# A fused transformer-like block: program parting moved to the end, more slack in the planned order, two blocks normalised on GpSimd

## The reference

```
h = tanh(xn @ W1.T + b1);  s = h @ w2.T + b2          # a score for each token
e = exp(s - max over the sequence)
ctx = cumsum(e * xn) / cumsum(e)                       # running mean along the sequence
attn = tanh(concat(ctx, xn) @ Wc.T + bc)
ffn = (silu(xn @ wg.T) * (xn @ wu.T)) @ wd.T           # wg, wu: 768 x 256, wd: 256 x 768
```

## Time and profile before

| | us |
|---|---|
| median of three runs | 396.42 |
| the profiled execution, whole | 396.52 |
| its span, first to last instruction | 394.3 |
| TensorE's first and last matmul | 1.5, 390.8 |
| flag written, branches on all engines | 67.9, 68.1 to 69.1 |
| VectorE busy, ScalarE busy, GpSimd busy | 296.4, 249.9, 192.2 |

### The profile page before, as it was taken

The page is one execution under the profiler, slowest core; times in us unless marked ns, Lnnn a source line. Parts: engine busy times, 40 slices in busy tenths (PEclk is TensorE's granted clock), DMA queues, the critical chain, the costliest instruction groups (busy, mean ns, idle before and its releaser), DMA issues.

```text
span 394.3 us, 7886 instructions
## 1 busy us (share of the span) xinstructions
PE 386.4 (98%) x2740; PEld 268.6 (68%) x2740; DVE 296.4 (75%) x632; ACT 249.9 (63%) x466; POOL 192.2 (49%) x257
## 2 busy tenths in 40 slices
PE   8999999999899999999999999999999999999996
PEld 4556676758566686777777776767677676676765
DVE  6799998999899989766848666788576765654351
ACT  4786898699787767797546836365463644536350
POOL 0535441273428997896825504947356555502000
PEclk9999999999999999999999999999999999999999
DMA  7933436037449324247330005142331330100001
GB/s 252 355 115 62 102 90 169 9 72 171 100 118 183 113 57 109 98 127 131 100 80 28 27 28 143 50 117 71 82 71 44 100 108 3 53 28 28 28 27 61
DMA packets 54946, 36.57 MB, mean 93 GB/s; under 512 B 31858, under 2 KB 50292, under 8 KB 54900
## 3 DMA queue, kind: packets, MB, share of 16 engines
q1 hardware_dynamic: 54608, 35.73, 34.0%
q10 hardware_dynamic: 292, 0.26, 0.2%
HBM read 20.19 MB, written 8.45 MB: 73 GB/s over the span
## 4 chain that ended last, share of the span: by engine, by line
PE 87%; DVE 6%; ACT 2%; issue 1%; SPq 1%; DMA 1%; POOL 0%; ACTq 0%; DVEq 0%; POOLq 0%
PE bank L686 41%; PE bank L722 36%; PE bank L742 8%; PE bank L1361 1%; SPq L1267 1%; DVE bank L1105 1%; DMA xres<-in_x 1%; DVE stats L940 1%; DVE ex L1110 1%; DVE bank L1090 1%; DVE veps L969 1%; ACT xt L838 1%; ACT xt L848 0%; DVE rstd L972 0%; DVE minus_half L970 0%
## 5 line engine op out<-in xcount | busy, mean ns | idle before, releaser
L722 PE MATMUL bank<-xt,narrow 128*128 128x512 f16 x768 | 177.8, 379 | 0.5 <-issue 0.5
L722 PEld LDWEIGHTS bank<-xt,narrow 128*128 128x128 f16 x768 | 75.1, 98 | 75.8 <-issue 1.0
L686 PE MATMUL bank<-narrow,wide 128*128 128x256 f16 x792 | 96.4, 273 | 0.0
L686 PE MATMUL bank<-narrow,xt 128*128 128x256 f16 x768 | 92.8, 273 | 0.0
L874 ACT ACTIVATE wide<-bank 128x512 f16<-128x512 f32 x90 | 53.6, 596 | 60.1 <-DVE bank L1105 59.7
L686 PEld LDWEIGHTS bank<-narrow,xt 128*128 128x128 f16 x768 | 75.1, 98 | 18.3 <-issue 0.4
L686 PEld LDWEIGHTS bank<-narrow,wide 128*128 128x128 f16 x792 | 77.5, 98 | 9.4
L1110 DVE TENSOR_TENSOR wide<-bank,wide 128x512 f16<-128x512 f32 x90 | 60.9, 683 | 25.1 <-ACT wide L874 24.2
L1105 DVE SCALAR_TENSOR_TENSOR bank<-bank,sg 128x512 f32<-128x512 f32 x96 | 66.1, 693 | 16.0 <-PE bank L722 15.6
L1235 POOL TENSOR_TENSOR wide<-ex,wide 128x512 f16<-128x512 f32 x32 | 39.4, 1246 | 78.8 <-ACT wide L888 78.7
L867 ACT ACTIVATE sg<-bank 128x512 f32<-128x512 f32 x96 | 56.7, 595 | 25.1 <-PE bank L722 24.2
(11 more groups left out here) (101 smaller groups left out, 263.9 us busy)
## 6 DMA issues: line engine op xcount, KB each, us to landing
rows<-scratch SPq DMA_DIRECT2D x16, 512.0 KB, 5.4
out_y<-xres SPq DMA_DIRECT2D x31, 256.0 KB, 2.2
xres<-in_x SPq DMA_DIRECT2D x15, 512.0 KB, 4.9
xt<-xt SPq DMA_TRANSPOSE x56, 2.5
wide<-in_wg SPq DMA_DIRECT2D x1, 768.0 KB, 6.5
wide<-in_wu SPq DMA_DIRECT2D x1, 768.0 KB, 8.9
wide<-in_wd SPq DMA_DIRECT2D x1, 768.0 KB, 10.6
wide<-in_wc SPq DMA_DIRECT2D x1, 512.0 KB, 11.8
```

The costliest lines, as they stand in the source:

```text
L686: return pe.matmul(dst, lhs, rhs, start=False, stop=stop, skip_group_check=True)
L722: mm = pe.matmul(b[:, :], pg.up(which, k, j), pg.xn(sx, k, tok), start=n == 0, stop=n == len(todo) - 1)
```

## The change

- The branch of an engine now waits in the plan for its last large step as well: D(15,2) on TensorE, Ct(15,2) on ScalarE, Da(15,0) on VectorE, Cl(15,1) on GpSimd, O(15,0) on SyncE. All steps may stand before it but Da and O of (15,1) and (15,2). The wide program repeats all, and loads all of x and all weights again (21 loads in place of 5).
- Steps Kg to Fl get due times from 215 on (they were 41 to 58) and come behind C(3,1); their copies lie in a part of `xt` that is free by then. K1 and Kc stay.
- In the plan, a result of another engine counts as seen 1.0 us later on TensorE and 0.3 us later on ScalarE, from 30 us on. On the engine that made it, it still counts 0.1 us sooner.
- Blocks 1 and 2 are normalised on GpSimd (new step Lp, a tensor_scalar with two per-partition factors), not on ScalarE.
- Load Lx(i) stands behind Tx(i-6), and counts as seen after 9.0 us; statistics are due 2 us sooner; block 2's x counts as there at 20.0.
- All orders are planned anew with this.

```diff
+SLACK, STEADY = {TE: 1.0, SE: 0.3}, 30.0
...
-    "T": (PO, 1.35, 1.45), "N": (PO, 3.2, 3.3), "Cl": (PO, 1.2, 1.3), "Xm": (PO, 1.5, 1.6),
+    "T": (PO, 1.35, 1.45), "N": (PO, 3.2, 3.3), "Cl": (PO, 1.2, 1.3), "Lp": (PO, 0.75, 0.85), "Xm": (PO, 1.5, 1.6),
...
-    "Lx": (SY, 0.6, 4.0), "Tx": (SY, 2.6, 4.8),
+    "Lx": (SY, 0.6, 9.0), "Tx": (SY, 2.6, 4.8),
...
+POOLED = (1, 2)
...
-X_SENT = (0.0, 11.1, 18.0)
+X_SENT = (0.0, 11.1, 20.0)
...
-AHEAD = ("Ln", "Lb", "Xh", "Xl", "Xm", "Tx", "Ss", "S", "Th", "Sv", "Gg", "Sg", "Gu", "H", "Hh", "Hl", "D", "Da")
+AGAIN = ("Ln", "Lp", "Lb", "Xh", "Xl", "Xm", "Tx", "Ss", "S", "Th", "Sv", "Gg", "Sg", "Gu", "H", "Hh", "Hl", "D", "Da",
+         "V0", "M1", "V1", "Ex", "M2", "V2", "M3", "V3", "Er", "Ro", "N", "Sc", "Ch", "Cl", "Cs", "C", "Ct", "Ca", "O")
+END = {TE: "D", SE: "Ct", VE: "Da", PO: "Cl", SY: "O"}
...
-                lead = 4.0 if i <= FIRST_T + 2 else 8.0
+                lead = 6.0 if i <= FIRST_T + 2 else 10.0
...
+            if i in POOLED:
+                due["Lp", i, pr] = due["Ln", i, pr]
...
+    for e, branch in BRANCH_OF.items():
+        if kind == branch:
+            return [(("Fl", 0, 0), 0), ((END[e], LAST, {TE: 2, SE: 2, VE: 0, PO: 1, SY: 0}[e]), 0)]
...
-        return [(("Tx", i - 5, 1), 0)] if i >= FIRST_T + 5 and not wide else []
+        return [(("Tx", i - 6, 1), 0)] if i >= FIRST_T + 6 and not wide else []
...
-    return kind in WEIGHTS + ONCE or (kind in AHEAD and i < BLK_SEQ - 1)
+    return kind in WEIGHTS + ONCE or (kind in AGAIN and not (kind in ("Da", "O") and st[1] == LAST and st[2]))
...
-            t = max(t, when - into - (0.1 if by == e else 0.0))
+            t = max(t, when - into + (-0.1 if by == e else SLACK.get(e, 0.0) if when > STEADY else 0.0))
...
-            return rows[:, :, :, :].rearrange("p r k t -> p (r k t)").bitcast(F16)[:, n * SHARE:(n + parts) * SHARE]
+            return xt[:, :].bitcast(F16).rearrange("p (c t) -> p c t", c=2 * KD)[:, n:n + parts, 2 * BLK:2 * BLK + SHARE]
...
+            elif kind == "Lp":
+                if i > FIRST_T + 1:
+                    pool.wait_ge(g_xm, pg.nth("Xm", i - 2, k))
+                elif i <= FIRST_T:
+                    pool.wait_ge(p_x, pg.nth("Lb", i - 1, k))
+                pool.wait_ge(*root_ready(i))
+                for t in range(2):
+                    c = 4 * i + 2 * k + t
+                    ins = pool.tensor_scalar(normed(pg, i, k)[:, t, :], xres[:, c, :], rstd[:, c:c + 1], shift[:, c:c + 1],
+                                             ALU.mult, ALU.add)
+                ins.then_inc(g_xn, 1)
```

More of the change, by code:

```diff
@@ L222, with norm @@
 DUE = due_times()
+def norm(i, wide):
+    return "Lp" if i in POOLED and not wide else "Ln"
 def needs(st, wide):
@@ L342, in __init__ @@
         self.earlier = {st[0]: 0 for st in DUE}
-        once = [st for st in earlier if st[0] in ONCE or st[0] not in AHEAD]
+        once = [st for st in earlier if st[0] in ONCE or st[0] not in AGAIN]
         for st in earlier:
@@ L351, in __init__ @@
         self.free = dict(BEGIN)
-        skip = {*self.done, *(st for st in DUE if not (st[0] not in WEIGHTS + ("Xm", "Tx") if wide else
+        skip = {*self.done, *(st for st in DUE if not (st[0] not in WEIGHTS + ("Xm", "Tx", "Lp") if wide else
                                                        st[1] < FIRST_T if st[0] in ("Lb", "Xl") else
                                                        st[1] >= FIRST_T if st[0] in ("Xm", "Tx") else
-                                                       st[:2] != ("Ln", 0)))}
+                                                       st[:2] != ("Ln", 0) and (st[0] not in ("Ln", "Lp") or st[0] == norm(st[1], wide))))}
         self.todo = {e: sorted((st for st in DUE if STEP[st[0]][0] == e and st not in skip), key=DUE.get)
@@ L585, in __init__ @@
                 self.plan = ANY if wide_operands else FITS
+                self.softmaxes, self.loads = (SEQS, NBLK // 2) if wide_operands else (0, 0)
                 if wide_operands:
@@ L799, in tensor_step, with through @@
                 mm.then_inc(p_m, 1)
+        def through(eng, pg):
+            eng.wait_ge(p_d, pg.plan.earlier["D"])
+            eng.wait_ge(a_y, pg.plan.earlier["Ct"])
+            eng.wait_ge(v_d, pg.plan.earlier["Da"])
+            eng.wait_ge(g_clo, pg.plan.earlier["Cl"])
         def tensor_program(pe, pg):
             if pg.wide:
[L804 to L811, removed]
+                through(pe, pg)
                 pe.wait_ge(a_32, 1)
@@ L914, in scalar_program @@
             if pg.wide:
[L915 to L925, removed]
+                through(act, pg)
                 act.wait_ge(s_again, 16 * len(again))
@@ L1149, in vector_step @@
                     dve.wait_ge(v_k2, 3)
-                dve.tensor_scalar(largest(first, n).bitcast(U16), w.bitcast(U16), NO_SIGN, None,
+                else:
+                    dve.wait_ge(p_y, pg.nth("C", 3, 1))
+                dve.tensor_scalar(largest(first, n).bitcast(U16), in_shares(w).bitcast(U16), NO_SIGN, None,
                                   ALU.bitwise_and).then_inc(v_k2, 1)
@@ L1182, in vector_program @@
             if pg.wide:
+                through(dve, pg)
                 dve.wait_ge(s_again, 16 * len(again))
-                dve.wait_ge(p_x, pg.plan.earlier["Lb"])
-                dve.wait_ge(p_u, pg.plan.earlier["Gu"])
                 dve.tensor_scalar(rstd[:, 0:4], rstd[:, 0:4], X_UP, None, ALU.mult).then_inc(v_rs0, 1)
@@ L1239, in pool_program @@
             if pg.wide:
+                through(pool, pg)
                 pool.wait_ge(s_again, 16 * len(again))
@@ L1289, in sync_program @@
             if pg.wide:
[L1290 to L1295, removed]
+                through(sp, pg)
+                sp.wait_ge(s_out, 16 * pg.plan.earlier["O"])
                 for dst, src in again:
@@ L1299, in sync_program @@
                 sync_step(sp, pg, kind, i, n)
-            sp.wait_ge(s_out, 16 * sum(len(shares(i)) for i in range(NBLK)))
+            sp.wait_ge(s_out, 16 * (pg.plan.earlier["O"] * pg.wide + sum(len(shares(i)) for i in range(NBLK))))
         def branch(eng, program, who):
@@ L1313, in block_kernel @@
         again = [(half(wg32.bitcast(I32)), rows_of(wg)), (half(wu32.bitcast(I32)), rows_of(wu)),
[L1314 to L1316 removed]
+                 (wd32.bitcast(I32).rearrange("p (k n) -> p k n", k=KH), rows_of(wd)),
+                 (w1_32, rows_of(w1)), (wc_32, rows_of(wc))]
+        again += [(xres[:, 4 * i:4 * i + 4, :], token_rows(x, i)) for i in range(NBLK)]
         @block.sync
```

68 lines of the change are left out of this document (35 added, 33 removed).

## The result

The changed kernel takes 393.59 us (median of 4 runs, 392.97 to 393.89), against 396.62 for the kernel before (4 runs). The ratio is 0.992, 95% interval 0.9903 to 0.9937, so it is 3.0 us (0.8%) faster. The forecast was 393.5, with a range from 392.4 to 395.9.

A forecast was written before the change was run, and what follows sets the result against it. TensorE, busy 98% of the span, was taken as the bound, with 3.68 us lost in listed gaps. Terms -0.69 - 1.3 - 1.2 + 0.3 = -2.9 took the median of 396.42 to 393.5 us; range 392.4 to 395.9.

The forecast's parts named there:

- The parting, -0.69: Programs' branching near 68 us: moving it to the end removes TensorE's whole 0.69 us gap there.
- Rival C: Kernel end: the way out gets longer through SyncE's larger other program, giving 395.8 us; chance 0.08.
- The sign set for C: Kernel end: more than 3.5 us behind the last matmul would show the forecast wrong; 3.3 us was expected.
- The 0 for the end: Kernel end: 0.95 us of moved branching is hidden behind other waits, so costs 0; at most 0.95 uncovered.
- Blocks 1 and 2 on GpSimd, -1.3: Gaps near 22 and 33 us: relieving ScalarE wins 1.3 of 0.97 + 0.65 us, at 0.40 us per GpSimd instruction.
- rival D: Early blocks: GpSimd's instruction costs much over 0.4 us; slower from 1.14, 399.1 us at the 1.48 bound; chance 0.07.
- The reading of D(0,0): First down-projection, near 33 us: its 0.27 and 0.38 us stops hang on Hh(0,5), behind ScalarE's block 2 normalising.
- VectorE and GpSimd in each other's way, 0: New GpSimd stretches, 19.4 to 21.0 and 27.6 to 29.2 us: they meet harmless VectorE work, so the sum is unchanged.
- Slack, -1.2: Gap before M1, first sequence's softmax, 99 to 102 us: slack wins 1.2 of 1.37 us; bounds 0 and 1.37.
- Loads, statistics and checks, 0: Checks moved to 215 us, 0 (0 to 0.5); loads six blocks behind and earlier statistics, 0 (-0.1 to +0.5).
- A new order, +0.3: All engines replanned: gaps not there now may open, costing 0.3 us (0 to 1.5).
- B: Rival, 20 to 60 us: VectorE is the bound and gaps move instead of closing, giving 395.3 us; chance 0.16.

The follow-up runs named there:

- no_part: The kernel before with slack, GpSimd normalising and changed loads and statistics, but branches and checks Kg to Fl left in place: 393.37 us, ratio 0.9921.
- slack_only: The kernel before with only the plan's slack added (1.0 us TensorE, 0.3 us ScalarE, from 30 us on): 396.39 us, ratio 0.9995.
- slack_loads: The kernel before with slack and the changed loads and statistics; branches and checks stay, ScalarE normalises: 393.83 us, ratio 0.9937.
- no_pooled: The changed kernel with blocks 1 and 2 normalised on ScalarE instead of GpSimd: 393.55 us, ratio 0.9920.
- pooled_only: The kernel before with only blocks 1 and 2 normalised on GpSimd: 396.68 us, ratio 1.0003.
- part_only: The kernel before with only the branches and checks Kg to Fl moved: 395.50 us, ratio 0.9976.
- loads_only: The kernel before with only loads six blocks behind, statistics due 2 us sooner and block 2's x counted from 20 us: 396.31 us, ratio 0.9988.
- no_slack: The changed kernel without the plan's slack: 397.44 us, ratio 1.0020.
- te_slack: The changed kernel with slack for TensorE alone, none for ScalarE: 394.25 us, ratio 0.9950.

## Why the prediction was right, and where it was not

Taken over the whole change, the frame was right: TensorE at its pace bounds the kernel, only the listed places could be won (3.68 us), and the net of 2.9 us is what TensorE's timeline shows (2.97). The split over the edits was wrong in nearly every term. That terms which do not hold one by one add up to within 0.1 us of the measured time is in part luck; what holds up is that the listed gaps behind 34 us close where the slack is there with the parting or the loads.

- **The parting, -0.69.** The gap went, but the move is not what it takes: it is worth 0 beside the other parts (no_part), and the gap also closes in slack_only and slack_loads, where the branch stays. TensorE had met it with too little queued. At the end, VectorE and SyncE part ahead of the last output as said, though with less room, since TensorE's last sums are in another order: VectorE idles 0.62 us there, not 1.93, and SyncE issues O(15,1) 0.34 us after its data, but the last output 0.04 after. TensorE's last jump took 3.7 us and its drain is at 391.1, VectorE's at 391.3, both ahead of SyncE's at 391.8, the end of the block in the changed kernel (source line L472):

```profile
L472 PEldq DRAIN  x1: 73/73/73, 391.1 to 391.1; - x1
L472 DVEq DRAIN  x1: 41/41/41, 391.3 to 391.3; - x1
L472 SPq DRAIN  x1: 38/38/38, 391.8 to 391.8; - x1
```

  Rival C did not come: SyncE's last branch at 391.3 has its drain 0.5 us on, as before. The sign set for C was a bad one: 3.7 us lie behind the end of the last matmul (388.4 to 392.1), over its bound of 3.5, but the kernel before has 3.5 too (390.8 to 394.3), not the 3.3 that the prediction took. The 0 for the end may be a little short. From the start of the last matmul to the end, the eight profiles with the parting at the end have 3.74 to 4.35 us (3.99 on average), the six with it in mid-kernel 3.56 to 3.86 (3.71). The cause of these 0.3 us is open.
- **Blocks 1 and 2 on GpSimd, -1.3.** The early gaps did close by about 1.0 net of the new 0.50, but other edits close them as well (no_pooled), and with this edit alone others open elsewhere (pooled_only). The price was mis-sized: 0.56 for 0.40, as the source line shows.

```profile
L1239 POOL TENSOR_SCALAR xnat<-xres,rstd,shift x8: 559/562/564, 20.1 to 30.1; 128x256 f32<-128x256 f32 x8
```

  So four took 2.19 us. That is far below the 1.14 each from which rival D decides. The line was drawn between two forms with constants, one of them from int32 to float16; whether the two factors per partition or the types make the difference, no run shows. Block 2 was ready at 30.7, or 30.1 without the longer start-up, and not at 29.2.

  The reading of D(0,0) was wrong in part. Its last stop (0.38) does not hang on Hh(0,5), which had ended at 31.88, but on Hl(0,5), VectorE's half of the same tile. That stood behind root steps that run beside GpSimd's two Xm operations of 31.03 to 33.30. VectorE's timeline before, 27 to 35.5 us:

```profile
31.40 0.81 DVE L969 TENSOR_SCALAR veps<-mv 128x4 f32<-128x4 f32 x1
32.24 1.08 DVE L970 TENSOR_SCALAR minus_half<-veps 128x4 f32<-128x4 f32 x1
...
33.63 0.69 DVE L1110 TENSOR_TENSOR ex<-bank,ex 128x512 f16<-128x512 f32 x1
```

  In the changed kernel Hh(0,5) starts at 31.24, not 2 us earlier than the 31.30 of before, and Hl(0,5) follows it at 31.85, since the root steps come later (34.71, 0.17 each). The first stop (0.27) the profile puts down to ScalarE's Sg, as the prediction's path by ScalarE would have it.
- **VectorE and GpSimd in each other's way, 0.** The step failed where it looked only at the new instructions. Those hold up nothing of note, but Wdh, pushed from 19.37 to 22.35, met a root step: the 0.50 above. The Trainium skill's rule that the prediction names (SBUF — State Buffer, Summary: rules for kernel authors), by which the later of two such instructions waits for the other's end, agrees with this trace (the root step ends at 23.85, Wdh at 23.82). Its application stopped one instruction short.
- **Slack, -1.2.** M1's 1.37 went, but in part_only, loads_only and no_slack M1 itself waits for nothing either, and 0.28 to 1.08 is lost just behind it. So the gap at M1 takes another order; that nothing opens beside it takes the slack. A term for one gap was the wrong model. The slack is worth 3.9 us beside the other three parts (397.44 to 393.59), 2.5 beside the loads (396.31 to 393.83), 1.7 beside the parting (395.50 to 393.85) and 0.2 alone. With one of these parts there, it is what keeps the gaps of a new order closed. Other amounts of slack were not tried.
- **Loads, statistics and checks, 0.** Right for the sum, but the 0 for the checks holds only with slack on ScalarE; without it their place comes with a stop of 0.56 us at 213 to 216 us (part_only, no_slack, te_slack), a little over the 0.5 that the prediction allowed. The checks were held up in their new place. In the changed kernel's groups from 200 to 250 us the same shapes that took 0.55 before read:

```profile
L1173 DVE TENSOR_TENSOR xt<-xt 128x768 f16<-128x768 f16 x1 | 1.5, 1506 | 0.0
L1163 DVE TENSOR_SCALAR xt<-narrow 128x1536 uint16<-128x1536 uint16 x1 | 1.3, 1259 | 0.0
```

  TensorE loses nothing there, so VectorE's idle time took it.
- **A new order, +0.3.** Behind 34 us the changed kernel lost 0.08, less than that. Without slack the new orders lost 1.3 to 3.6 us there (part_only, loads_only, pooled_only, no_slack), and slack_only 1.9, where before lost 2.06. I gave B 0.16 and a bad order 0.05. The four single parts show that this was the real risk: one gap closed, another opened, and no gain clear of noise in three of four.

## What to carry to other kernels

In a statically ordered kernel whose longest engine is full, a stall seen in the trace belongs to the order, not to the edit that removes it: price the order's tolerance to late operations first, and expect edits made one at a time to show little. Count the late operations as well, since the plan's costs do not know them. The branch in mid-kernel cost TensorE only what its queued matmuls did not cover. When an instruction moves to another engine, follow what it pushes there as well as what it meets.

## What was not expected of the hardware

- A TENSOR_SCALAR of 256 columns with two factors per partition takes 0.56 us on GpSimd (the changed kernel), where the same work took 0.60 as an activation on ScalarE (before).
- Beside GpSimd, a VectorE step of 4 columns took 0.85 instead of 0.17, and one of 768 columns with both inputs in SBUF 1.51 instead of 0.55 (both in the changed kernel). In the kernel before such waits come to 7.3 us in the root steps alone, and each of the nine ends within 0.05 us of a GpSimd operation's end.
